# Causal mask of the row maxima as extra contraction rows, in a fused linear-attention, softmax-attention and FFN block

## The reference, cut to what matters

```python
# x: (8, 512, 128) float32
x = x + deltanet(layernorm(x))     # linear attention with decay, a scan over time, 8 heads
x = x + ffn(layernorm(x))          # product with sign(weight)
x = x + attn(layernorm(x))         # softmax attention, 16 heads of 8 features, rotary, causal:
    scores = einsum('bhsd,bhtd->bhst', q, k) * scale
    scores = where(t > s, finfo.min, scores)
    probs  = softmax(scores, axis=-1); ctx = einsum('bhst,bhtd->bhsd', probs, v)
x = x + ffn(layernorm(x))
```

## Time and profile before

| | us |
|---|---|
| median of 3 runs | 749.57 |
| lowest, highest | 744.65, 756.94 |
| the profiled execution, its own time | 753.01 |
| its span in the trace | 750.9 |

### The profile page before, as it was taken

One profiled execution on the slowest core, in us unless ns is written; L12 is line 12 of the kernel. 1 busy time (PEld: TensorE's weight loads), 2 busy tenths in 40 slices (PEclk: granted clock), 3 DMA queues, 4 the chain that ended last, 5 costly groups with the idle time before them and its releaser, 6 DMA issues.

```text
span 750.9 us, 17433 instructions
## 1 busy us (share of the span) xinstructions
PE 653.8 (87%) x6640; PEld 375.3 (50%) x6670; DVE 563.3 (75%) x1571; ACT 426.4 (57%) x900; POOL 187.8 (25%) x231
## 2 busy tenths in 40 slices
PE   3666767889999999999999999999999998899885
PEld 2334435445554655555646554556555545356333
DVE  4675673788976988899888879896899678768302
ACT  2543642545686558746775568465866563563750
POOL 4241640244043313422134212241243110100000
PEclk9689896599999999999999999999999999999985
DMA  3000026000450044002700161014301340540000
GB/s 107 1 1 1 16 69 101 2 17 2 87 100 1 17 98 89 2 10 66 113 17 24 52 99 29 2 58 76 55 9 56 63 64 17 96 75 3 16 1 14
DMA packets 20934, 32.37 MB, mean 43 GB/s; under 512 B 3178, under 2 KB 18282, under 8 KB 18538
## 3 DMA queue, kind: packets, MB, share of 16 engines
q1 hardware_dynamic: 20850, 31.25, 21.2%
HBM read 22.46 MB, written 8.39 MB: 41 GB/s over the span
## 4 chain that ended last, share of the span: by engine, by line
PE 55%; DVE 24%; issue 8%; ACT 7%; DMA 3%; POOL 2%; SPq 1%; DVEq 0%; ACTq 0%; POOLq 0%
PE ps L1066 8%; PE ps L1021 8%; PE ps L1051 8%; DVE mrow L1491 7%; PE ps L795 5%; PE ps L869 3%; DVE qkf L1460 3%; PE ps L896 3%; PE ps L1053 3%; DVE am L1335 3%; PE ps L1023 2%; PE ps L790 2%; PE ps L916 2%; ACT pT L762 2%; PE ps L905 2%
## 5 line engine op out<-in xcount | busy, mean ns | idle before, releaser
L1491 DVE TENSOR_REDUCE mrow<-ps 128x1 f32<-128x384 f32 (+3 forms) x352 | 221.4, 634 | 78.5 <-PE ps L1023 76.0
L762 ACT ACTIVATE pT<-ps 128x512 f32<-128x512 f32 (+1 forms) x352 | 186.9, 558 | 105.1 <-PE ps L1053 101.6
L1021 PE MATMUL ps<-ks,qs 72*128 72x512 bf16 (+3 forms) x512 | 140.0, 309 | 17.3 <-DVE mrow L1491 14.1
L1051 PE MATMUL ps<-qs,ks 75*128 75x256 bf16 (+3 forms) x512 | 131.5, 305 | 4.1 <-DMA qs<-mT 2.5
L1023 PE MATMUL ps<-cbf 128*128 128x128 bf16 x512 | 101.5, 224 | 0.0
L1066 PE MATMUL ps<-pT,va 128*32 128x512 f32 (+3 forms) x1024 | 96.1, 451 | 5.3 <-ACT pT L762 5.0
L1021 PEld LDWEIGHTS ps<-ks,qs 72*128 72x128 bf16 x512 | 50.3, 99 | 96.0 <-DVE mrow L1491 78.2
L1053 PE MATMUL ps<-cbf 128*128 128x128 bf16 x512 | 98.0, 221 | 0.0
L546 POOL TENSOR_TENSOR spread<-state,cst 128x144 f32<-128x144 f32 x112 | 47.5, 445 | 186.8 <-DVE state L1364 153.2
L1051 PEld LDWEIGHTS ps<-qs,ks 75*128 75x128 bf16 x512 | 50.5, 99 | 76.0 <-ACT pT L762 30.6
L534 POOL TENSOR_TENSOR xe<-lpart,hot 96x1024 bf16<-96x1024 bf16 x32 | 60.3, 1893 | 47.8 <-DVE lpart L1321 47.8
(11 more groups left out here) (189 smaller groups left out, 1092.6 us busy)
## 6 DMA issues: line engine op xcount, KB each, us to landing
ks<-scratch SPq DMA_DIRECT2D x48, 192.0 KB
scratch<-parts SPq DMA_DIRECT2D x48, 128.0 KB, 1.7
qs<-scratch SPq DMA_DIRECT2D x32, 128.0 KB
qs<-scratch SPq DMA_DIRECT2D x16, 192.0 KB
x<-x SPq DMA_DIRECT2D x8, 256.0 KB, 3.1
qs<-scratch SPq DMA_DIRECT2D x32, 64.0 KB
out<-xk SPq DMA_DIRECT2D x8, 256.0 KB, 2.4
qs<-mT SPq DMA_DIRECT2D x48, 8.0 KB
```

The source lines that it names most:

```text
L762: act.activation(pT[:, c0:c0 + m, P_OFF[kt]:P_OFF[kt] + width], ps[:, score_banks(b)[n % len(score_banks(b))], 0:m * width].rearrange("p ( ...
L1021: pe.matmul(o, qs[0:K_MAX, f % RING, h, qt * P:(qt + 1) * P], ks[0:K_MAX, f % RING, h, 0:width], start=True, stop=False, skip_group_check= ...
L1051: pe.matmul(o, ks[0:K_ALL, place, h, kt * P:(kt + 1) * P], qs[0:K_ALL, place, h, kt * P:T], start=True, stop=False, skip_group_check=True)
L1491: dve.tensor_reduce(mrow[:, qt, h0:h0 + m], ps[:, max_banks(b)[n % len(max_banks(b))], 0:m * width].rearrange("p (m k) -> p m k", k=width) ...
```

## The change

The mask of the maxima is no longer a product of its own. `qs` and `ks` get 43 more rows (`MARKS`, rows 75 to 117, `K_DIAG` = 118) that hold, for a query and a key within a tile of 128, powers of two whose products sum to a small value where the key is allowed and to a very negative one where it is not. The product of the diagonal 128x128 tile runs over 118 rows; the part left of it (qt > 0) is a product of its own over 72 rows. For this, queries and keys are held at 2**-32 (scaled into the rotary tables) and the exponential's scale undoes it. Rows 72 to 74 of `qs` must be zero in the maxima, so each stack ends with one more DMA from a zero row of a constant (`zeros`). The marks are built once: six DVE instructions, two PE transposes, one ACT copy to `pT`, and six DMAs from `pT`, one for each of `qs` and `ks` at three places, of 43 rows by 8 copies of 1 KB. Transposed scores (L1051, L1053) are unchanged. The order strings differ in every engine, mostly by a step or two.

```diff
-N_STACK = 16 * (len(Q_COPIES) + len(K_COPIES))
+N_STACK = 16 * (len(Q_COPIES) + len(K_COPIES) + 1)
+SMALL = 2.0 ** -32
+MARKS = (P + 2) // 3
+K_DIAG = K_ALL + MARKS
+MARK = (2.0 ** -87, 2.0 ** -12, 2.0 ** 63)
...
-SP_ORDER = "nnmmmmmmmmnxmmmmmmmxnmxmmmammmxnmmxmmammmmxnmmmxmmmmamxmnxmammmmmmxmmxmmmmammxmxmmmmmmamxmxxaa"
+SP_ORDER = "nnxmmmmmmmmnxmmmmmmmxnmxmmmmmmamxnmmxmammmmxmnmxmmmammmxnmmmxammmmmxmmxmmmmmamxmxmmmmmmmaxmxaxa"
...
+    marks_tok = pT[:, 2, 0:MARKS].bitcast(BF16).rearrange("p (s r) -> p s r", s=2)
+    marks = pT[0:MARKS, 3, 0:T].bitcast(BF16).rearrange("p (s t) -> p s t", s=2)
+    zeros = consts_bf[0:1, 2 * P:3 * P].unsqueeze(1).broadcast_to([PARTS, HH * C, P])
@@ SP, at the end of the eight stack copies of one f
+    sp.dma_start(qs[K_MAX:K_ALL, f % RING, :, :].rearrange("p h (c t) -> p (h c) t", t=P), zeros
+                 ).then_inc(stacked[f % RING], 16)
@@ SP, maxima(0)
+    sp.wait_ge(marks_ready, 1)
+    for place in range(RING):
+        for side, dst in enumerate((qs, ks)):
+            sp.dma_start(dst[K_ALL:K_DIAG, place, :, :],
+                         marks[:, side, :].unsqueeze(1).broadcast_to([MARKS, HH, T])
+                         ).then_inc(marks_in[place], 16)
@@ ACT, mid(0); sinT the same
-    act.activation(cosT[:, :], ps[:, BK_MID, :], ACT.Copy).then_inc(cos_sb, 1)
+    act.activation(cosT[:, :], ps[:, BK_MID, :], ACT.Copy, scale=SMALL).then_inc(cos_sb, 1)
@@ ACT, maxima(0)
+    act.wait_ge(marks_ps, 1)
+    act.activation(marks.rearrange("p s (c t) -> p s c t", c=C),
+                   ps[0:MARKS, BK_MAX, :].bitcast(BF16)[:, 0:2 * P].rearrange("p (s t) -> p s t", s=2)
+                   .unsqueeze(2).broadcast_to([MARKS, 2, C, P]), ACT.Copy).then_inc(marks_ready, 1)
@@ PE, before the first maxima group of f
+    if f < RING:
+        pe.wait_ge(marks_in[f], 32)
+        pe.wait_ge(ones_in[f], 16)
@@ PE, one head of a maxima group
-    pe.matmul(o, qs[0:K_MAX, f % RING, h, qt * P:(qt + 1) * P], ks[0:K_MAX, f % RING, h, 0:width],
-              start=True, stop=False, skip_group_check=True)
-    mm = pe.matmul(o[:, qt * P:(qt + 1) * P], ident_bf, future_qk,
-                   start=False, stop=True, skip_group_check=True)
+    own_tile = slice(qt * P, (qt + 1) * P)
+    if qt > 0:
+        pe.matmul(o[:, 0:qt * P], qs[0:K_MAX, f % RING, h, own_tile],
+                  ks[0:K_MAX, f % RING, h, 0:qt * P], start=True, stop=True, skip_group_check=True)
+    mm = pe.matmul(o[:, own_tile], qs[0:K_DIAG, f % RING, h, own_tile],
+                   ks[0:K_DIAG, f % RING, h, own_tile], start=True, stop=True, skip_group_check=True)
@@ DVE, maxima(0), for k = 0 and for k = 1, 2
+    ins = dve.tensor_scalar(to, columns, mark, None, ALU.mult)
+    ins = dve.scalar_tensor_tensor(to, columns, mark, to, ALU.mult, ALU.add)
```

More of the change, by code:

```diff
@@ L26 @@
 SCALE = 1.0 / math.sqrt(DA)
-NEG = -3.0e38
+NEG = -2.0 ** 60
 W_Q, W_K, W_V = 0, 128, 256
@@ L86 @@
 PE_ORDER = (
[L87 to L96, removed]
@@ L100 @@
+    "aaaxaaaaaaaaaaaaaaaaaaaaaaaaaaaaaaaaaaaaaaaaaaaaaaaaa"
 )
 ACT_ORDER = (
[L102 to L105, removed]
@@ new lines @@
+    "aasaaaasmaaaaaaaxasssasaaaaasaassaamsaassssaasssasaaaasaaasamaaamasxsssssamssasaamaaaaamamasnaaaasmaaaas"
+    "asxaassamaassasaaasaasssaaasasassaamsaamaaasaamaaaasmasxsssssaasmaasasaamaaanasaaaaaaamaasaaxaaassaaaasa"
+    "smaasaassaasassssasassaasaaaaamsamsaaaxsmsamssassaamamaasaaaasnsaaaaaasaaamaxasaaaaaasaassasaaamssaasaas"
+    "aasaaasssaaassasaamasxmssamsamsassssamamaasaaasasaaaaaasxaaamaaaaaaaaaamaaaaaaaaaaaaamamaaaaaaxmammaaaaa"
+    "maaaaaaaaaaaaaaaaxaaaaaaaaaaaaaaaaaaaaaaaaaaaxaaaaaaaaaaaaaaaaaaaxaaaaaaaaaaaaaaaaaaaaaaaaaaaaaaaaaa"
@@ L116 @@
[L116 to L120, removed]
@@ L258, in hybrid_block @@
         x_in = sem("x_in")
-        ones_in = sem("ones_in")
+        ones_in = [sem("ones_in%d" % place) for place in range(RING)]
         cleared = sem("cleared")
@@ L341, in hybrid_block @@
         stacked = [sem("stacked%d" % place) for place in range(RING)]
+        marks_ps = sem("marks_ps")
+        marks_step = sem("marks_step")
+        marks_ready = sem("marks_ready")
+        marks_in = [sem("marks_in%d" % place) for place in range(RING)]
         max_step = sem("max_step")
@@ L373, in hybrid_block @@
         ident = cst[:, C_ID:C_ID + P]
+        after = cst[:, C_AFTER:C_AFTER + P]
         tri = cst[:, C_TRI:C_TRI + P]
@@ L434, in _ @@
             for place in range(RING):
-                sp.dma_start(ks[K_MAX:K_ALL, place, :, :], ones[:, 0:HH, :]).then_inc(ones_in, 16)
+                sp.dma_start(ks[K_MAX:K_ALL, place, :, :], ones[:, 0:HH, :]).then_inc(ones_in[place], 16)
             def norm(b):
@@ L708, in mid @@
                     act.wait_ge(cos_ps, 1)
-                    act.activation(cosT[:, :], ps[:, BK_MID, :], ACT.Copy).then_inc(cos_sb, 1)
+                    act.activation(cosT[:, :], ps[:, BK_MID, :], ACT.Copy, scale=SMALL).then_inc(cos_sb, 1)
                     yield
                     act.wait_ge(cos_ps, 2)
-                    act.activation(sinT[:, :], ps[:, BK_MID, :], ACT.Copy).then_inc(cos_sb, 1)
+                    act.activation(sinT[:, :], ps[:, BK_MID, :], ACT.Copy, scale=SMALL).then_inc(cos_sb, 1)
                     yield
@@ L756, in attn @@
                         width = T - kt * P
+                        if n == 0 and b == 0:
+                            for place in range(RING):
+                                act.wait_ge(marks_in[place], 32)
                         if g >= 1:
@@ L763, in attn @@
                                        ps[:, score_banks(b)[n % len(score_banks(b))], 0:m * width].rearrange("p (m n) -> p m n", n=width),
-                                       ACT.Exp, scale=SCALE).then_inc(probs_ready, 1)
+                                       ACT.Exp, scale=SCALE / SMALL ** 2).then_inc(probs_ready, 1)
                         if g >= 1 and k == 2:
@@ L997, in maxima @@
                 banks = max_banks(b)
+                if b == 0:
+                    yield
+                    pe.wait_ge(masks_in, 16)
+                    pe.wait_ge(marks_step, 6)
+                    for side in range(2):
+                        mm = pe.transpose(ps[0:MARKS, BK_MAX, :].bitcast(BF16)[:, side * P:(side + 1) * P],
+                                          marks_tok[:, side, :], ident_bf)
+                    mm.then_inc(marks_ps, 1)
                 for f in (2 * b, 2 * b + 1):
@@ L1484, in maxima @@
             def maxima(b):
+                if b == 0:
+                    yield
+                    dve.wait_ge(consts_in, 16)
+                    for k in range(3):
+                        n = len(range(k, P, 3))
+                        for side, (table, mark) in enumerate(((ident, -MARK[2 - k]), (after, MARK[k]))):
+                            to, columns = marks_tok[:, side, 0:n], table[:, k:P:3]
+                            if k == 0:
+                                ins = dve.tensor_scalar(to, columns, mark, None, ALU.mult)
+                            else:
+                                dve.wait_ge(marks_step, 2 * k)
+                                ins = dve.scalar_tensor_tensor(to, columns, mark, to, ALU.mult, ALU.add)
+                            ins.then_inc(marks_step, 1)
                 s = Steps(max_step, b * MAX_STEPS)
```

53 lines of the change are left out of this document (33 added, 20 removed).

## The result

The changed kernel takes 801.93 us (median of 4 runs, 799.58 to 806.68), the kernel before in the same comparison 749.8. The ratio is 1.0728, with a 95% interval of 1.0647 to 1.0809: 7% slower. The profiled execution took 802.45 us with a span of 800.3.

The account below looks back on a forecast made before the run. The prediction took TensorE to bound the middle, with VectorE close behind. Against the profiled 753.01 us, +73 stall, +1 startup, +3 zero rows and -16 saving make 814, or 810 us at the runs' median; range 785 to 930.

Parts of the forecast that it names:

- The decisive step: Marks' DMAs on SP: 43 rows go to one engine, so the first stack is issued at 182 instead of 108.59 us.
- the signs it named: TensorE gap until some 195 us, DMA share near 0.06, six marks issues near 79, stack after 160, maxima waiting less.
- The rivals about the marks: Marks' DMAs: hidden over many engines, 738 us, chance 0.15; or one engine at 102 ns a packet, 930 us, chance 0.20.
- Size of the stall: Before the first maxima: six marks DMAs of 16.5 us, 99 us in all, delay everything by +73 us.
- The term of the packet: Marks' DMAs: one 1 KB packet on one engine takes 48 ns, from the stores' rate.
- The 40 ns end of its range: Low packet price, from the first loads: six marks DMAs 83 us, delay 56, total 785 us.
- Its high end, 102 ns: High packet price, from the stacks' rate: six marks DMAs 211 us, delay 187, total 930 us.
- The saving: Maxima on TensorE: 512 mask products go, 18.0 us of them on the path; 16 us taken, ends 14 and 22.
- Startup and zero rows: First normalisation's DVE steps and two transposes add 1 us; zero rows ending each stack add 3, between nothing and 6.
- The third rival: Zero rows come late at every stack, 0 to 1.5 us at 16 stacks, 24 us at most; within the range, no chance given.
- The clock: TensorE's restarted 48 us: if the clock stays at half instead of 0.74, up to 19 us more, within the range.
- The other price of a product: TensorE products: the skill page's 81 ns per 128 columns saves 16.8 us; the trace's 0.06 us, kept, saves 29.7.

Follow-up runs that it names:

- rows44: The changed kernel with the marks at 44 rows instead of 43, the 44th zero: 743.06 us, ratio 0.9873 to the kernel before.
- copies_alone: The kernel before plus six copies of 43 rows, which no product reads, at the marks' place on SP's queue: 814.46 us, ratio 1.0817.
- nomask_neworder: The kernel before without the mask product in the maxima (causal mask left out there), with the changed kernel's order strings: 741.51 us, ratio 0.989.
- before_neworder: The kernel before with the changed kernel's order of steps, without the marks' step: 755.17 us, ratio 1.0049.
- fat48: As wide48, with heads and tokens of each stack's copies written as one dimension: 740.31 us, ratio 0.9884 to the kernel before.
- wide48: As rows48, with each stack's zero rows read as three contiguous rows of 8 KB instead of 96 pieces of 256 bytes: 740.41 us, ratio 0.9883.
- rows48: The changed kernel with the marks at 48 rows instead of 43, five of them zero: 743.51 us, ratio 0.9882 to the kernel before.
- nomask: The kernel before without the mask product in the maxima (causal mask left out there), order of before: 745.91 us, ratio 0.9921.

## Why the prediction was right, and where it was off

**The decisive step held.** Forecast 810 us, measured 801.93. Most of the signs it named are there: the idle TensorE until 188 us that ends with a stack's copy, the DMA share of 0.07, the stack's issue after 160. Two are not. The six issues are not near 79 us but spread from 79.67 to 151.45, because SP is held at each; so the stores wait in SP and not, as the prediction had it, in the engine's queue, at the same cost. And the maxima groups do not wait less: TensorE stood 16.6 us before L1072 for a row maximum, where it stood 14.1 before L1021. The rivals about the marks fell. They were not hidden: rows44 shows what that would have been, 0.9873 or 740 us, where the rival had 738. And the packet did not cost 102 ns.

**Size of the stall.** Expected +73, from 6 x 16.5 = 99 us at 48 ns a packet. The copies follow each other every 14.89 us, 43.3 ns for each of 344 packets. Put into the prediction's own sum this is 80 + 89.3 + 2.3 + 1 (the landing after SP was let go) = some 173 us for the stack's issue, and it was 173.90. The term of the packet was 10% too high (48 for 43.3), and that is 10 of the 12 us by which the stall was missed (61.5 us by copies_alone, 61.3 between the traces of the kernel after and rows44). The 40 ns end of its range was a little nearer than the value taken. Its high end, 102 ns, came from the stacks, whose packets are of 8 KB and not of 1 KB; it was a price per KB.

**The saving.** Expected 16 us, measured 8.3 (nomask_neworder, 5.0 to 11.4 by its interval). The step that failed is the choice "I take 16, with 14 and 22 as ends": the share on the chain was taken nearly whole, though the same paragraph names VectorE as the path that could take over. VectorE's share of the chain did rise, from 24% to 30%, and in the old order the landing of the stacks came with it, which the prediction held to have "time left" at twelve stacks because TensorE's weight loads had waited for them only 2.0 us. Four waits of 0.5 us, 0.7 at most, mean that the margin is near nothing at those four stacks, not that it is comfortable at the others.

How much of the shortfall these paths explain is open. From the first maxima product to the end the traces have 628.7 us (before), 628.1 (before_neworder) and 626.5 (copies_alone) with the mask products, and 610.7 to 614.3 (fat48, after, rows44, wide48) with the marks in their place: there 14 to 18 us are won, about what was predicted. rows48 has 743.2 - 122.06 = 621.1 with the same work, so no single pair of traces can carry such a number. What these kernels lose again stands in front: without the stall, their first product starts at 126.5 to 128.1 us (fat48, rows44, wide48) where before has 122.23 and rows48 122.06. The prediction had 1 us for that. As nomask, whose front is that of before, starts at 125.45, the runs don't tell the order's part in it from the spread between executions.

**Startup and zero rows.** Expected +1 and +3. In the new order rows48 and nomask_neworder differ by nothing, so both are under the resolution. In the old order they cost, with the marks, 1.0024 - 0.9921 = 1.0%, 7.7 us. The third rival (zero rows late at each stack) may hold there in part, but that isn't shown: five stack landings are on that chain, and as many are on that of rows48. That the zero rows could be this cheap or dear by order alone was not in the prediction, which gave the order no term but a share in the upper end.

**The sum.** The two errors have opposite signs: 73 - 61.5 = 11.5 us too much stall, and 12 us of net gain expected where rows44 and rows48 show 9.6 and 8.9. Their difference, some 9 us, is the distance of the forecast from the result. The parts add up: 749.8 + 61.5 - 9.2 = 802.1. The clock, for which up to 19 us were allowed within the range, did not show: it was 0.5 through the hole, but 0.84 in the 48 us behind it, where rows44 has 0.83 without a hole.

**The other price of a product.** "Back-to-back issue gap" in the Trainium skill's TensorE: Matmul & The Clock Gate would, as the prediction reckoned, have taken 16.8 us off TensorE where the row takes 29.7. TensorE's busy time fell by 19.4 us in the kernel after and 19.9 in rows44 (653.8 to 634.4 and 633.9), between the two; as busy time includes the drain, this doesn't tell one from the other, and the time won, 8 us, is below either. The row still holds behind the change: four products of 128 columns in a row start at 193.94, 194.00, 194.06 and 194.12 us.

## What to carry to other kernels

Before a DMA is added, factor its number of rows: one row of padding (44 for 43) took 64 us off this kernel, and a copy nobody reads costs as much as one that matters when it stands ahead of the stores on the same queue. A share on the chain is a ceiling for a saving, not its value: look for the second path, and read small waits of the bottleneck for a DMA as a margin already used up. An order written out by hand belongs to the work it was made for; test the new work with the old order and the old work with the new before either is credited.

## What the runs showed of the hardware

SyncE's own instruction stream is held while one DMA engine still has earlier copies to drain. The first 43-row copy took 0.81 us to issue, the second 11.10, every later one 14.8 to 15.1, as long as one copy takes to drain; the six stores behind them took 17.30 us to issue where they took 6.68. Nothing of the stores moves on the other engines meanwhile, though they are spread over all of them:

```profile
160.00:165.00 5.00, 0.00 (x0) 0.00 (x0) 0.00 (x0) 0.00 (x0) 0.00 (x0) 0.50 0.07 24
...
167.00:168.00 1.00, 0.00 (x0) 0.00 (x0) 0.00 (x0) 0.00 (x0) 0.00 (x0) 0.50 0.81 265
```

The price of a 1 KB piece between SBUF rows depends on which engines write beside it. One engine alone moved 24 GB/s, 43 ns a piece. Sixteen moved 149 GB/s, 9.3 each or 110 ns. Eleven moved 172 GB/s, 65 ns on average, but not evenly: near the end of the copies rows44 has this row.

```profile
92.00:98.00 6.00, 5.54 (x74) 3.02 (x78) 3.07 (x8) 3.85 (x11) 4.16 (x7) 1.00 0.37 71
```

About six engines are still at work there, at 12 GB/s each or 85 ns. In the packet records of this trace the pieces fall into two groups, near 46 and near 86 ns, and only the second is left at the end. So the number of engines alone does not set the price; what the six have in common was not found. The six copies took 18.6 us from the first issue to the last piece both over eleven engines and over sixteen, and were over 3 us before the first store of `parts`. rows44's copies left SP after 1.99 us each from the third on, rows48's after 2.5 to 3.1. The stacks' rate at which the prediction put its high end, 10.0 GB/s an engine, is that of many engines at once (rows48's marks have 9.3), not a price of the kind of row.
